# A macaron block (FFN, selective scan, FFN): two of four convolutions to TensorE, the block output added by VectorE, other slots for the side work, five states of 16 weighed by GpSimd

## What is computed

```python
xn = resid * rsqrt(mean(resid * resid) + eps) * norm_w
skip, x = xn @ skip_w.T, xn @ in_w.T                       # 512 channels each
xc = conv_b + sum(xp[:, k:k+L, :] * conv_w[:, k] for k in range(4))   # xp: x behind 3 zeros
x = silu(xc)
delta = softplus((x @ wd1.T) @ wd2.T + wd2_b)
Bm, Cm = x @ wB.T, x @ wC.T                                # 16 states
h = exp(delta * A) * h + (delta * x) * Bm;  y = sum_n h * Cm          # a scan over 1024 tokens
out = resid + ((y + W_D * x) * silu(skip)) @ out_w.T
```

## Time and profile before

| what | us |
|---|---|
| median of 3 runs (lowest to highest) | 1326.85 (1325.11 to 1328.06) |
| the profiled execution's own time | 1325.21 |
| its span | 1323.4 |
| VectorE busy in the span | 1184.1 (89%) |
| TensorE busy | 1061.0 (80%) |
| GpSimd busy | 872.6 (66%) |
| ScalarE busy | 774.8 (59%) |
| VectorE's closings at slot 1 of segments 2 and 3 start at | 464.66 and 576.66 |
| first scan of segment 0 starts at | 224.78 |
| last closing (`finish`) of segment 7 starts at | 1132.95 |

### The profile page before, as it was taken

One profiled execution on the slowest core, in us unless ns is written; L12 is line 12 of the kernel. 1 busy time (PEld: TensorE's weight loads), 2 busy tenths in 40 slices (PEclk: granted clock), 3 DMA queues, 4 the chain that ended last, 5 costly groups with the idle time before them and its releaser, 6 DMA issues. The chain is left out here.

```text
span 1323.4 us, 10922 instructions
## 1 busy us (share of the span) xinstructions
PE 1061.0 (80%) x2688; PEld 456.6 (35%) x2688; DVE 1184.1 (89%) x1768; ACT 774.8 (59%) x1321; POOL 872.6 (66%) x390
## 2 busy tenths in 40 slices
PE   3999746687889788888878988987897867799973
PEld 2434212233343343334334333432432422444421
DVE  3765898999999999999999999999999999576587
ACT  2656658757456566745666664665674434265665
POOL 0000004889989999998999999899999999000000
PEclk9999978799999999999989989999998889899998
DMA  6000003244543535343444444445444443000003
GB/s 207 1 1 1 1 1 113 96 160 133 170 141 130 181 112 185 127 159 128 149 169 141 165 142 149 140 126 191 139 149 162 137 177 112 0 1 1 1 1 128
DMA packets 48000, 146.56 MB, mean 111 GB/s; under 512 B 5504, under 2 KB 14336, under 8 KB 47936
## 3 DMA queue, kind: packets, MB, share of 16 engines
q1 hardware_dynamic: 47440, 145.03, 33.1%
q10 hardware_dynamic: 496, 0.82, 0.2%
HBM read 141.05 MB, written 4.72 MB: 110 GB/s over the span
## 5 line engine op out<-in xcount | busy, mean ns | idle before, releaser
L1155 POOL TENSOR_TENSOR late<-m_dx,m_brow 128x1024 f32<-128x1024 f32 x256 | 597.7, 2363 | 6.7 <-DVE m_a_bank L1285 6.5
L957 ACT ACTIVATE m_a_bank<-m_delta,m_negA 128x512 f32<-128x512 f32 x512 | 335.1, 683 | 174.6 <-DVE m_hc L1297 134.0
L1442 PE MATMUL m_y_bank<-m_hc,ident 128*128 128x512 f32 x640 | 332.4, 645 | 116.1 <-DVE m_hc L1297 115.4
L1167 POOL TENSOR_TENSOR m_hc_pool<-m_hid,m_crow 128x1024 f32<-128x1024 f32 x96 | 226.8, 2363 | 31.0 <-DVE m_hid L1285 30.6
L1442 PEld LDWEIGHTS m_y_bank<-m_hc,ident 128*128 128x128 f32 x640 | 119.6, 201 | 305.1 <-DVE m_hc L1297 186.7
L1297 DVE TENSOR_TENSOR m_hc<-m_a_bank,m_crow 128x512 f32<-128x512 f32 x320 | 203.0, 677 | 0.0
L1285 DVE TENSOR_TENSOR_SCAN m_a_bank<-m_a_bank,m_carry,late 128x512 f32<-128x512 f32 x160 | 196.4, 1274 | 1.1 <-ACT m_a_bank L957 0.8
L1285 DVE TENSOR_TENSOR_SCAN m_a_bank<-m_a_bank,late 128x512 f32<-128x512 f32 x160 | 186.7, 1212 | 7.0 <-ACT m_a_bank L957 3.7
L1442 PE MATMUL m_y_bank<-m_hc_pool,ident 128*128 128x512 f32 x384 | 188.0, 613 | 4.9 <-POOL m_hc_pool L1167 4.9
L1176 POOL TENSOR_TENSOR m_dx<-m_delta,m_x 128x1024 f32<-128x1024 f32 x16 | 38.0, 2377 | 216.5 <-ACT m_delta L1047 216.5
L1285 DVE TENSOR_TENSOR_SCAN m_hid<-m_a_bank,m_carry,late 128x512 f32<-128x512 f32 x96 | 117.7, 1269 | 0.0
(11 more groups left out here) (148 smaller groups left out, 1237.9 us busy)
## 6 DMA issues: line engine op xcount, KB each, us to landing
m_brow<-bc_rows SPq DMA_DIRECT2D x128, 512.0 KB, 5.0
m_crow<-bc_rows SPq DMA_DIRECT2D x128, 512.0 KB, 4.1
x_tok<-x_in SPq DMA_DIRECT2D x4, 1024.0 KB, 8.6
out<-x_tok SPq DMA_DIRECT2D x3, 1024.0 KB, 4.8
...
```

The costliest lines, as they stand in the source:

```text
L957: nc.scalar.activation(a_bank[K % 2][:, j, :], delta[:, i % 2, c, :], ACT.Exp, scale=negA[:, c, n:n + 1]).then_inc(S["a"], 1)
L1155: nc.gpsimd.tensor_tensor(u[:, K % U_RING, :, :], dx[:, i % 2, 2 * q:2 * q + 2, :], brow[:, K // 2 % ROW_RING, K % 2, :].unsqueeze(1).to_b ...
L1167: nc.gpsimd.tensor_tensor(hc_pool[:, before % POOL_RING, :, :], hid[:, before % POOL_RING, :, :], crow[:, K // 2 % ROW_RING, K % 2, :].uns ...
L1442: op = nc.tensor.matmul(y_bank[:, j, :], ident[:, :], source[:, before % ring, j, :], start=False, stop=K % PASS == PASS - 1)
```

## The change

The states whose products GpSimd weighs go from six of 16 (0, 2, 5, 7, 10, 12) to five (0, 3, 6, 9, 12). For segments 1 to 7 blocks 2 and 3 are convolved by TensorE: ScalarE copies the projection to `raw`, behind its last three columns of the half before, and TensorE multiplies four shifted views of it with four diagonal matrices; silu then reads PSUM and adds the bias. `out` is added straight from PSUM by VectorE. The slots of nearly all side work move. The B and C rows are stored at row 13 of the segment in place of 9. VectorE's last statistics stand ahead of its last two additions. Five small products of `norms` become `scalar_tensor_tensor` with a 1.0.

```diff
-    POOL_N = (0, 2, 5, 7, 10, 12)
+    POOL_N = (0, 3, 6, 9, 12)
+    PE_CONV = (2, 3)
     PLACES = {
         "in": ((0, 0), (1, 1), (3, 3), (4, 4)),
         "out": ((6, 6), (7, 7)),
-        "xproj": ((10, 10),),
-        "skip": ((11, 11), (14, 14), (19, 19), (20, 20)),
-        "dt": ((13,), (15,), (16,), (17,)),
-        "turn": ((24,), (25,)),
+        "skip": ((9, 9), (10, 10), (24, 24), (25, 25)),
+        "taps": ((), (), (12, 12, 13, 13), (13, 13, 14, 14)),
+        "xproj": ((18, 18),),
+        "dt": ((20,), (21,), (22,), (23,)),
+        "turn": ((27,), (28,)),
     }
     AT = {
         "acc": (2, 3, 5, 6),
-        "silu": (8, 8, 8, 8),
-        "out_there": (9, 10),
-        "proj": (12,),
-        "tanh_s": (13, 16, 21, 22),
-        "step": (15, 17, 18, 19),
-        "softplus": (20,),
-        "xn_tok": (23, 24),
-        "xn": (26, 27),
-        "z": (28, 29),
-        "conv": (2, 3, 5, 6),
-        "gate": (13, 16, 21, 22),
+        "tanh_s": (11, 12, 26, 27),
+        "silu": (17, 17, 17, 17),
+        "proj": (20,),
+        "step": (22, 23, 24, 25),
+        "softplus": (25,),
+        "xn_tok": (25, 26),
+        "xn": (29, 30),
+        "z": (30, 31),
+        "conv": (2, 3),
+        "out_add": (8, 9),
+        "gate": (11, 12, 26, 27),
         "finish": (1, 17),
-        "dx": (23, 24),
-        "out_add": (13, 14),
+        "dx": (28, 29),
     }
...
+                if c in PE_CONV and p > 0:
+                    nc.scalar.activation(raw[:, c - 2, 0:TAPS - 1], none[:, :] if ph == 0 else raw[:, c - 2, BANK:],
+                                         ACT.Copy).then_inc(S["history"], 1)
+                    act.wait_ge(S["history"], 2 * (p - 1) + c - 1)
+                    nc.scalar.activation(raw[:, c - 2, TAPS - 1:], b, ACT.Copy).then_inc(S["raw"], 1)
+                    return
...
+                if c in PE_CONV and p > 0:
+                    nc.scalar.activation(x[:, p % 2, c, :], work_there((i, "taps", c)), ACT.Silu,
+                                         bias=conv[:, c, TAPS:TAPS + 1]).then_inc(S["x"], 1)
+                    return
...
-            def take_out(i, c):
-                b = work_there((i, "out", c))
-                act.wait_ge(S["gated"], i * KE)
-                nc.scalar.activation(th[:, c, :], b, ACT.Copy).then_inc(S["out_there"], 1)
...
+            for c in PE_CONV:
+                for s in range(TAPS):
+                    op = nc.vector.tensor_scalar(diag_w[:, c - 2, s, :], ident[:, :], w512[:, c, o + s:o + s + 1], None,
+                                                 ALU.mult)
...
-                    nc.vector.tensor_tensor(square, rstd[:, ts], rstd[:, ts], ALU.mult).then_inc(S["square"], 1)
+                    nc.vector.scalar_tensor_tensor(square, rstd[:, ts], 1.0, rstd[:, ts], ALU.mult, ALU.mult)\
+                        .then_inc(S["square"], 1)
...
+            def out_add(i, c):
+
+                dve.wait_ge(S["work_done"], USES.index((i, "out", c)) + 1)
+                dve.wait_ge(S["z"], 2 * i)
+                at = (i - 1) * HT + 2 * c
+                to = x_tok[:, at:at + 2, :].rearrange("p a d -> p (a d)")
+                nc.vector.tensor_tensor(to, to, bank_of((i, "out", c)), ALU.add).then_inc(S["out_added"], 1)
...
+                elif kind == "taps":
+                    if part == 0:
+                        pe.wait_ge(S["diag_w"], 1)
+                        pe.wait_ge(S["raw"], 2 * p + c - 1)
+                    op = nc.tensor.matmul(b, diag_w[:, c - 2, part, :], raw[:, c - 2, part:part + BANK],
+                                          start=part == 0, stop=part == TAPS - 1)
```

More of the change, by code:

```diff
@@ L797, in exists @@
     def exists(i, kind):
-        return {"out": puts_out(i), "skip": core(i), "turn": turns(i)}.get(kind, prep(i))
+        return {"out": puts_out(i), "skip": core(i), "turn": turns(i), "taps": prep(i) and i >= 0}.get(kind, prep(i))
     def bank_name(i, kind, c, index):
@@ L825, in released @@
         p = i + 1
-        if use[:2] == (-1, "in"):
+        if kind == "in" and p == 0 and c not in PE_CONV:
             return "spill", c + 1
-        return {"turn": ("xn", 2 * p + c + 3), "out": ("out_there", 2 * (i - 1) + c + 1), "in": ("conv", KE * p + c + 1),
+        if kind == "in" and p > 0 and c in PE_CONV:
+            return "raw", 2 * p + c - 1
+        return {"turn": ("xn", 2 * p + c + 3), "out": ("out_added", 2 * (i - 1) + c + 1), "in": ("conv", conv_count(p, c)),
+                "taps": ("x", KE * p + c + 1),
                 "xproj": ("proj", p + 1), "dt": ("step", KE * p + c + 1), "skip": ("gated", KE * i + c + 1)}[kind]
@@ L866, in mamba @@
         one_col = sb("one_col", [P, 1])
+        raw = sb("raw", [P, 2, TAPS - 1 + BANK])
+        diag_w = sb("diag_w", [P, 2, TAPS, P])
+        none = sb("none", [P, TAPS - 1])
         xn_tok = tmp_u[:, 0:2, :].rearrange("p a (b d) -> p (a b) d", d=DIM)
@@ L875, in mamba @@
             "negA", "expA", "late_by_dve", "late_straight", "late_added", "late_stats", "moments", "root", "square", "rstd", "diag_d", "final_stats", "constants",
-            "xn_tok", "xn", "z", "work_done", "acc", "taps", "spill_part", "spill", "conv", "x",
+            "xn_tok", "xn", "z", "work_done", "acc", "history", "raw", "none", "diag_w", "taps", "spill_part", "spill", "conv", "x",
             "proj", "bc_stored", "tanh_s", "gated", "step", "delta", "dx0", "dx1",
             "brow0", "brow1", "brow2", "crow0", "crow1", "crow2",
-            "u", "a", "scan", "carry", "hc", "hc_pool", "y_dve", "y_pool", "y", "out_there", "out_added")}
+            "u", "a", "scan", "carry", "hc", "hc_pool", "y_dve", "y_pool", "y", "out_added")}
         block = ctx.enter_context(nc.Block())
@@ L1014, in accumulate @@
                     lo = TAPS - 1
-                    act.wait_ge(S["spill"], p // 2 * KE + c + 1)
+                    act.wait_ge(S["spill"], p // 2 * 2 + c + 1)
                     for j in range(lo):
@@ L1132, in _ @@
                         deviation(n)
-                for c in due(k, "out_there") if puts_out(i) else ():
-                    take_out(i, c)
                 if prep(i):
@@ L1310, in keep_spill @@
             def keep_spill(i, c, s):
-                b, done = bank_of((i, "in", c)), (i + 1) // 2 * KE * 2 + c * 2
+                b, done = bank_of((i, "in", c)), (i + 1) // 2 * 2 * 2 + c * 2
                 if s == 1:
@@ L1341, in convolve, with final_measure @@
                         keep_spill(i, c, s)
+            def out_add(i, c):
[4 more added lines that the diff above has]
+                nc.vector.tensor_tensor(to, to, bank_of((i, "out", c)), ALU.add).then_inc(S["out_added"], 1)
+            def final_measure():
+                dve.wait_ge(S["out_added"], 2 * 2 * HALVES)
+                for t in range(2 * BT):
+                    op = nc.vector.bn_stats(final_stats[:, t, :], x_tok[:, t, :])
+                op.then_inc(S["final_stats"], 1)
+                dve.wait_ge(S["final_stats"], 1)
+                for t in range(2 * BT):
+                    nc.vector.bn_aggr(moments[:, t, :], final_stats[:, t, :])
             def gate_skip(i, c):
-                if c == 0 and puts_out(i):
-                    dve.wait_ge(S["out_there"], 2 * i)
                 dve.wait_ge(S["tanh_s"], i * KE + c + 1)
@@ L1348, in gate_skip @@
                                                ALU.add, ALU.mult).then_inc(S["gated"], 1)
-            for K in range(-UNITS, TOTAL + 2):
+            for K in range(-UNITS, TOTAL + UNITS):
                 i, k = K // UNITS, K % UNITS
@@ L1364, in _ @@
                         convolve(i, c)
+                if K == TOTAL + 2:
+                    final_measure()
+                for c in due(k, "out_add") if puts_out(i) else ():
+                    out_add(i, c)
                 for c in due(k, "gate") if core(i) else ():
@@ L1367, in _ @@
                 if K == AT["conv"][-1] - UNITS:
-                    for c in range(KE):
+                    for c in PE_CONV:
+                        convolve(i, c)
+                    for c in range(KE - len(PE_CONV)):
                         keep_spill(-1, c, 1)
@@ L1374, in _ @@
                     norms(1, K // 10)
-            dve.wait_ge(S["out_added"], 2 * 2 * HALVES)
-            for t in range(2 * BT):
-                op = nc.vector.bn_stats(final_stats[:, t, :], x_tok[:, t, :])
-            op.then_inc(S["final_stats"], 1)
-            dve.wait_ge(S["final_stats"], 1)
-            for t in range(2 * BT):
-                nc.vector.bn_aggr(moments[:, t, :], final_stats[:, t, :])
         @block.tensor
```

40 lines of the change are left out of this document (20 added, 20 removed).

## The result

The changed kernel took 1339.74 us in the median of 4 runs (1333.76 to 1341.03), the kernel before 1326.42 on the same chip: a ratio of 1.0092 [1.0064, 1.0119], **slower by 0.9%**. The profiled execution took 1333.76 us, the fastest of the four; its span is 1332.0. The runs spread by 7 us, where those of before spread by 3. Why that is, turned out to be where the forecast went wrong. So I keep a second profiled execution of the same kernel beside the first all the way, 1339.7 us (span 1337.9), which is nearly the median.

The account below looks back on a forecast made before the run. VectorE was taken as the bound, GpSimd nearly a second. Work -5.3, vanished waits -12.2, ends -2.5 and new waits +38.8 gave +18.8 us on the profiled 1325.2: 1344 us, range 1328 to 1350 or 1351.

Parts of the forecast that it names:

- Work of VectorE: All segments: one state more per pass, two convolutions less in segments 0 to 6, addition of `out` at 0.6: -5.3 us.
- ends: Before segment 0 two spills less, -1.3 us; at the kernel's end an earlier last addition, -1.2; together -2.5.
- `norms`: Small VectorE operations in segment 0, now `scalar_tensor_tensor`: no change taken, between -4.2 and +2.3 us.
- the 48 of the forecast: Taps on TensorE, 16 records a segment at 0.43 us in seven segments: TensorE up 48 us, hidden.
- Waits that go: VectorE's middle-layer waits behind ScalarE's exponentials, GpSimd's u and a tanh disappear: -12.2 us, if nothing takes their place.
- The wait at unit 26: VectorE waits at slot 26 for ScalarE's group: 3.3 us in even segments, 2.5 in odd, plus 1.6 from late `dt`.
- The silu term: Silus at slot 17 need 7.5 us against 6.85: a wait of 0.6 us in even segments, none in odd.
- the table load: ScalarE's table switches in the slot 25 group: 1.3 us kept; the skill page's price would add some 19 us.
- so I expect the low clock again: TensorE idles some 3 us before pass 2's feed-through: x-projection's copy 0.8 us late (even), unit 26's group 1.6 late.
- rival B: TensorE's clock stays high at the feed-through: new waits 26.7 us, total +6.7, 1332 us; chance 0.25.
- if the feed-through of pass 2 takes 2 us: Sign on TensorE's feed-through that the forecast is wrong and rival B holds.
- Rival C: The group at slot 25 is covered, only 2.4 us of new waits left: -17.6 us, 1308 us; chance 0.12.

Follow-up runs that it names:

- e2: Changed kernel with softplus two slots later (27, not 25) and dx at 29 and 30: 1314.67 us, ratio 0.9907.
- e9: Changed kernel with the four small products of norms as tensor_tensor again: 1336.76 us, ratio 1.0078.
- e3: Changed kernel with xn_tok one slot later (26 and 27), turn and xn one slot later too, softplus left: 1331.96 us, ratio 1.0031.
- e7: e2 plus two or three unread matmuls at slot 17 that keep TensorE busy ahead of the feed-through: 1309.67 us, ratio 0.9875.
- e8: Changed kernel with softplus at 27, six states on GpSimd and unread matmuls keeping TensorE busy ahead of the feed-through: 1297.14 us, ratio 0.977.

## Why the prediction was right, and where it wasn't

The forecast was 1344 us, slower; measured were 1339.7 and 1340.0, inside the range and on the side given. As a difference it's further off: the sum was +18.8, and the medians of the kernel before and the changed one differ by 13.3 (1339.7 - 1326.4). The sum was added to the profiled execution of before, which lies 1.2 us under the median, and that hides a part.

- **Work of VectorE:** -5.3 forecast, -5.5 measured. The measured one also holds what the forecast counted under ends and `norms` (the spills less, 1.7 us of diagonals more, 1.1 less for `norms`), so the match is partly luck. The addition of `out` takes 671 ns in its group, 0.6 by the spacing. GpSimd's 819.2 and TensorE's rise (37.8 and not 48) are near enough. The 112 new records at 0.43 are the 48 of the forecast. The missing 10 are in other records that took less: the feed-throughs 35.6 us for 41.2, the sums 514.7 for 520.4.
- **Waits that go:** the rows on GpSimd and the tanh are gone, as forecast. That e2 has 4.8 us in all behind exponentials bears out that the old waits came from the places and not from a limit of ScalarE.
- **Ends:** the tail from the last closing to the last addition was 10.55 us and is 9.3, -1.2 as forecast. The head, from VectorE's first operation of the middle layer to its first scan, gave 1.1 of 1.3: 224.78 - 188.57 = 36.2 us before, 224.21 - 189.10 = 35.1 after. The taps start 13.75 us behind that operation in both, and the missing 0.2 is a short wait among them, behind ScalarE. That the first scan is only 0.6 us earlier by the clock of the trace comes from the FFN ahead, which ended 0.5 later. The eight diagonals took 1.7 us, inside time in which VectorE waited anyway (that wait is 1.2 us now and was 2.8).
- **`norms`:** no change was right; e9 shows it.
- **The wait at unit 26:** the mechanism and its size were right. With the clock high I had 3.3 + 0.75 = 4.05 in even segments, measured 4.07; in odd ones 3.1, where the same terms would give 2.5 + 0.75 = 3.25, measured 3.47. In the even ones two small errors cancel: the exponentials of unit 25 ended 2.71 us after T (543.84 + 1.30 - 542.43), so 0.98 late and not 0.75, and from there to the scan it was 7.12 us and not 7.27. The silu term, 0.6, is 0.62. e2 shows that this group is the cause, and e3 that its pieces add up. About the table load I had kept to the row: the load of 1.28 us at 545.76 is followed by the softplus 0.02 us after its end, here as before. The Trainium skill (ScalarE: Activation LUTs, "What ACT_TABLE_LOAD costs") has 2.66 us for a switch; 7.18 us for the whole group leaves no place for that.
- **The step that failed** is the one that reads "so I expect the low clock again", in all seven segments: a lateness of 1.6 us at unit 26 and 0.8 behind the x-projection's copy. I had read one feed-through of before, segment 2, and carried it to all. Even segments never lost the clock (idle 1.86 us, 1.98 each time, in both executions); odd ones did in one segment of three or in all three. Forecast and rival B were both true, segment by segment: 38.8 us of new waits by the one, 26.7 by the other, 29.8 and 35.3 measured. That mis-sized term is 3.5 to 9 us, and it accounts for the 4 us by which the median lies under the forecast. Its price was off too. Where the clock fell, the wait at unit 26 grew by 0.82 (4.29 for 3.47), as forecast (0.85). But behind the copy I had 0.8 in even segments and nothing in odd ones, and it was the odd ones that waited, 0.78 where the feed-through took 2.5 or 3.0 us, 1.97 and 1.94 where it took 3.78. By the prediction's own sign ("if the feed-through of pass 2 takes 2 us") the first profiled execution is rival B's: six of seven took 2 us, and its 1333.8 us lies 2 from B's 1332 and 10 from 1344. That the median came out nearer the forecast depends on how often the clock fell in odd segments, which nothing in the prediction foresaw; that much of the hit is luck.

The trace of before would have warned me. Its feed-throughs of segments 3 and 4, TensorE's timeline:

```profile
640.50 1.98 PE L1430 MATMUL m_y_bank<-m_x,m_diag_d 128*128 128x512 f32 x4 [2.29 <-DVE m_gate L1307]
...
752.25 3.42 PE L1430 MATMUL m_y_bank<-m_x,m_diag_d 128*128 128x512 f32 x4 [1.92 <-DVE m_gate L1307]
```

One is fast after 2.29 us of idle time and one slow after 1.92. The clock was a matter of the segment and of the execution, not of the kernel, and its rows have to be read together.

Rival C's price (1308) was for a group that is covered. The kernel with that cover, e2, took 1314.7 with the clock still falling, and e7 1309.7 with it high. Beside their own kernels before, that is 13.0 us faster with the two entries alone and 17.0 with the busy matmuls as well. So the change's idea held 13 to 17 us, and its table of slots spent all of it and 13 more.

What stays open: why TensorE's clock falls in some executions and not in others after the same 3.3 us, and what the two rows of e8 that remain (4.0 and 3.0 us) would need.
